# Capsule routing in a convolution kernel: one added on the scalar engine, exponentials behind copies, uniform votes behind pool taps, the ninth tap summed last in eight slots

## The reference

```python
def squash(s, axis=-1):
    n2 = jnp.sum(s * s, axis=axis, keepdims=True)
    return s * n2 / ((1.0 + n2) * jnp.sqrt(n2 + EPS))
...
    patches = patches.reshape(N, F_in, in_len, Ho, Wo, kh, kw)           # 4 input capsules of 8, 3x3 taps
    priors = jnp.einsum('nfdhwij,ofijud->nhwofiju', patches, weight)     # 4 output capsules of 8
    priors = priors.reshape(N, Ho, Wo, F_out, F_in * kh * kw, out_len)
    logits = jnp.zeros_like(priors)
    for r in range(3):
        probs = jax.nn.softmax(logits, axis=-3)                          # over the 4 output capsules
        out = jnp.sum(probs * priors, axis=-2, keepdims=True)
        if r != 2:
            out = squash(out)
            logits = logits + jnp.sum(priors * out, axis=-1, keepdims=True)
    out = squash(jnp.squeeze(out, axis=-2))
```

## Time and profile before

| | |
|---|---|
| median of 3 runs | 12398.2 us (12397.93 to 12406.01) |
| profiled execution: time, span | 12399.53 us, 12397.7 us |
| routing phase | first matmul of L708 at 85.7 us, last transfer out issued at 3824.76 us |
| busy over the span | PE 11867.1 us (96%), DVE 8639.8 (70%), ACT 7576.8 (61%), POOL 3955.4 (32%) |
| mean granted clock of TensorE | 0.987 of full speed |

### The profile page before, as it was taken

How to read it: one execution, slowest core, us unless ns; L and a number is a source line. 1 busy time by engine, 2 the same in 40 slices (tenths; PEclk the granted TensorE clock), 3 DMA queues, 4 the chain that set the end, 5 groups by cost and what they waited for, 6 DMA issues and landing times. The chain is left out here.

```text
span 12397.7 us, 255720 instructions
## 1 busy us (share of the span) xinstructions
PE 11867.1 (96%) x72764; PEld 4295.5 (35%) x72764; DVE 8639.8 (70%) x15928; ACT 7576.8 (61%) x15666; POOL 3955.4 (32%) x3876
## 2 busy tenths in 40 slices
PE   6999999999994999999999999999999999999899
PEld 2333333333331333333333333333333333333232
DVE  6777777777776777777777777777777777777300
ACT  4666666666662466666666666666666666666511
POOL 5777777777772010100101101011010010110144
PEclk9999999999996899999999999999999999999999
DMA  3110110110104333333333333333333333433365
GB/s 81 24 23 17 24 23 17 24 23 17 24 16 108 68 79 76 88 73 83 83 72 88 75 82 83 76 84 78 77 88 73 83 82 74 88 77 77 90 146 125
DMA packets 971114, 833.12 MB, mean 67 GB/s; under 512 B 669476, under 2 KB 703876, under 8 KB 960132
## 3 DMA queue, kind: packets, MB, share of 16 engines
q1 hardware_dynamic: 968196, 807.54, 29.6%
q10 hardware_dynamic: 1536, 8.39, 0.3%
HBM read 584.08 MB, written 229.48 MB: 66 GB/s over the span
## 5 line engine op out<-in xcount | busy, mean ns | idle before, releaser
L1616 DVE TENSOR_REDUCE a_big<-a_mp 128x1 f32<-128x512 f32 x8192 | 5181.0, 684 | 1933.2 <-PE a_mp L1453 1930.3
L1539 ACT ACTIVATE a_ex<-a_sc 128x512 f32<-128x512 f32 x8192 | 4393.9, 601 | 1718.6 <-PE a_sc L1441 1715.8
L1453 PE MATMUL a_mp<-a_ks,a_qs 108*128 108x512 bf16 x8192 | 3131.2, 383 | 40.1 <-DMA a_ks<-qk_parts 26.2
L1441 PE MATMUL a_sc<-a_qs,a_ks 111*128 111x512 bf16 x8192 | 3124.8, 383 | 45.4 <-issue 27.3
L928 DVE TENSOR_TENSOR r_prod<-r_pg,r_win 128x512 f32<-128x512 f32 x2816 | 1821.7, 684 | 775.5 <-PE r_pg L641 465.6
L550 POOL TENSOR_TENSOR r_prod<-r_temp,r_win 128x512 f32<-128x512 f32 x1792 | 2093.0, 1187 | 704.6 <-ACT r_temp L871 610.7
L1467 PE MATMUL a_po<-a_ex,a_va 128*32 128x512 f32 x16384 | 2216.7, 606 | 11.7 <-issue 6.3
L1441 PEld LDWEIGHTS a_sc<-a_qs,a_ks 111*128 111x128 bf16 x8192 | 795.8, 97 | 2593.0 <-ACT a_ex L1539 1747.0
L1352 POOL TENSOR_TENSOR a_on<-a_oc,a_zb 128x512 f32<-128x512 f32 x256 | 325.5, 1272 | 3508.3 <-DMA a_zb<-z_rows 3508.3
L1340 POOL TENSOR_TENSOR a_pieces<-a_left,a_pieces 128x512 bf16<-128x512 f32 x256 | 296.0, 1156 | 2900.4 <-ACT a_pieces L1525 2900.4
L871 ACT COPY r_temp<-r_pg 128x512 f32<-128x512 f32 x1792 | 976.8, 590 | 329.1 <-PE r_pg L641 207.8
(11 more groups left out here) (191 smaller groups left out, 10943.4 us busy)
## 6 DMA issues: line engine op xcount, KB each, us to landing
a_qs<-qk_parts SPq DMA_DIRECT2D x768, 144.0 KB
a_ks<-qk_parts SPq DMA_DIRECT2D x768, 144.0 KB
qk_parts<-a_pieces SPq DMA_DIRECT2D x128, 768.0 KB, 5.0
f_t<-mixed SPq DMA_DIRECT2D x48, 1536.0 KB, 16.1
a_tw<-second SPq DMA_DIRECT2D x512, 128.0 KB, 3.5
a_zb<-z_rows SPq DMA_DIRECT2D x256, 256.0 KB
mixed<-a_t SPq DMA_DIRECT2D x256, 256.0 KB, 5.8
r_win<-first SPq DMA_DIRECT2D x128, 280.5 KB, 5.0
```

Source lines behind the costliest of these rows:

```text
L1441: pe.matmul(sc[k % BANKS][:, :], ks[0:KROWS + NPART, p.h, head, 128 * kb:128 * kb + 128], qs[0:KROWS + NPART, p.h, head, CHUNK * qb:CHUNK ...
L1453: pe.matmul(mp[k % BANKS][:, :], qs[0:KROWS, p.h, head, 128 * q:128 * q + 128], ks[0:KROWS, p.h, head, CHUNK * half:CHUNK * half + CHUNK], ...
L1539: nc.scalar.activation(ex[:, k % RING, :], sc[k % BANKS][:, :], ACT.Exp, scale=scale).then_inc(exped.sem, 1)
L1616: nc.vector.tensor_reduce(big[:, x % 2, k // 2:k // 2 + 1], mp[k % BANKS][:, :], AX_X, ALU.max).then_inc(maxed.sem, 1)
```

## The change

It has four parts:

1. In the slots outside `FULLER` PE sums batch 2 ahead of batch 1, so tap 8 is last (`last_batches`); `when_summed` gives DVE and POOL the count to wait for before they overwrite a product.
2. In the squashes of rounds 1 and 2 ACT adds one to the squared norm, in part B ahead of Ln. DVE does reciprocal and ratio in part B, right ahead of L981, where they were in part A (`divide`). The uniform squash keeps its order on DVE.
3. The exponential of a softmax moves on ACT from the end of the slot of part A to part B, the slot after it, behind the copies of taps 4 and 5.
4. `first_votes` moves on POOL behind the products of taps 6 and 0 in slot 14. ACT's repeat of the first lane's vote moves from the end of slot 14 into slot 15, behind Ln and Exp and ahead of the copy out.

```diff
+def last_batches(s):
+    return (1, 2) if s % SLOTS in FULLER else (2, 1)
+
+def when_summed(s, g):
+    b = next(k for k, gs in enumerate(BATCHES) if g in gs)
+    return 3 * s + (1 + last_batches(s).index(b) if b else 0) + 1
...
@@ POOL
-            pool.wait_ge(reduced.sem, reduced.at(p.n, 3 * (s - 2) + batch_of[g] + 1))
+            pool.wait_ge(reduced.sem, reduced.at(p.n, when_summed(s - 2, g)))
...
-                elif r == 0:
-                    first_votes(n)
-                else:
+                elif r > 0:
                     scale_capsules(n, r, lane)
...
             for n, kind, r, lane in lit:
                 if kind == "softmax":
                     probabilities(n, r, lane)
+                elif r == 0:
+                    first_votes(n)
...
@@ PE
-                batch(behind.n, (s - 1) % SLOTS, 1)
-                batch(behind.n, (s - 1) % SLOTS, 2)
+                for b in last_batches(s - 1):
+                    batch(behind.n, (s - 1) % SLOTS, b)
...
@@ ACT
+                if r:
+                    nc.scalar.activation(fac[:, own, ls, :], norm[:, own, ls, :], ACT.Identity,
+                                         bias=one[:, 0:1]).then_inc(plus1[r].sem, 1)
                 nc.scalar.activation(lnorm[:, own, ls, :], norm[:, own, ls, :], ACT.Ln,
...
-            for d, kind, r, lane, part in lights(s, "B", ("squash",)):
+            for d, kind, r, lane, part in lights(s, "B"):
                 if d in which:
                     first_functions(p.to(d).n, kind, r, lane)
+            for d, kind, r, lane, part in back:
+                if r == 0 and lane == 0:
+                    repeat_votes(p.to(d).n, 0, 0)
...
-                if d in which and kind == "softmax":
-                    first_functions(p.to(d).n, kind, r, lane)
-                elif d in which and r == 0:
+                if d in which and kind == "squash" and r == 0:
                     uniform_capsules(p.to(d).n)
...
@@ DVE
+        def divide(n, r, lane):
+            k = lane + 1
+            nm, fc = (tile[:, int(r > 0), lanes_of(r, lane), :].rearrange("p l x -> p (l x)") for tile in (norm, fac))
+            dve.wait_ge(plus1[r].sem, plus1[r].at(n, k))
+            nc.vector.reciprocal(fc, fc).then_inc(recip[r].sem, 1)
+            dve.wait_ge(recip[r].sem, recip[r].at(n, k))
+            nc.vector.tensor_tensor(fc, fc, nm, ALU.mult).then_inc(ratio[r].sem, 1)
...
-                dve.wait_ge(normed[r].sem, normed[r].at(n, k))
-                nc.vector.tensor_scalar(fc, nm, 1.0, None, ALU.add).then_inc(plus1[r].sem, 1)
-                fill()
-                dve.wait_ge(plus1[r].sem, plus1[r].at(n, k))
-                nc.vector.reciprocal(fc, fc).then_inc(recip[r].sem, 1)
-                fill()
-                dve.wait_ge(recip[r].sem, recip[r].at(n, k))
-                nc.vector.tensor_tensor(fc, fc, nm, ALU.mult).then_inc(ratio[r].sem, 1)
+                if r == 0:
+                    dve.wait_ge(normed[r].sem, normed[r].at(n, k))
+                    nc.vector.tensor_scalar(fc, nm, 1.0, None, ALU.add).then_inc(plus1[r].sem, 1)
+                    divide(n, r, lane)
                 return
...
+            if r:
+                divide(n, r, lane)
```

More of the change, by code:

```diff
@@ L387, in routing_phase @@
     eps = sb("eps", [128, 1])
+    one = sb("one", [128, 1])
     prod = sb("prod", [128, TAPS, CHUNK])
@@ L418, in routing_phase @@
     pt = ctx.enter_context(nc.psum_tensor("r_pt", [128, CHUNK], F32))
-    batch_of = {g: b for b, gs in enumerate(BATCHES) for g in gs}
     fixed = sem("fixed")
@@ L682, in batch @@
                         last = pe.matmul(pl[C * q:C * q + C, cols], ws[:, 8, :], product_at(s, 8)[:, cols],
-                                         start=False, stop=False, tile_position=(0, C * q))
+                                         start=False, stop=b == last_batches(s)[1], tile_position=(0, C * q))
                 last.then_inc(reduced.sem, 1)
@@ L690, in batch @@
                     last = pe.matmul(pl[q:q + 32, :], ws[:, tap, :], rhs, start=b == 0,
-                                     stop=b == 2, tile_position=(0, q))
+                                     stop=b == last_batches(s)[1], tile_position=(0, q))
                 else:
@@ L780, in tail @@
         def tail(p):
-            batch(p.to(-1).n, SLOTS - 1, 1)
-            batch(p.to(-1).n, SLOTS - 1, 2)
+            for b in last_batches(SLOTS - 1):
+                batch(p.to(-1).n, SLOTS - 1, b)
         run_slots(pe, passes, slot, tail)
@@ L844, in second_functions @@
                 nc.scalar.activation(rz[:, lane, :], lz[:, lane, :], ACT.Exp, scale=-1.0).then_inc(rz_ready[r].sem, 1)
-            elif r < 2:
+            elif r == 1:
                 repeat_votes(n, r, lane)
@@ L905, in slot @@
             for d, kind, r, lane, part in lights(s, "A"):
-                if d in which and kind == "softmax":
-                    first_functions(p.to(d).n, kind, r, lane)
-                elif d in which and r == 0:
+                if d in which and kind == "squash" and r == 0:
                     uniform_capsules(p.to(d).n)
-                elif d in which:
+                elif d in which and kind == "squash":
                     square(p.to(d).n, r, lane)
@@ L920, in _ @@
         dve.wait_ge(fixed, 16 * 9)
+        nc.vector.memset(one[:, :], 1.0)
         nc.vector.memset(eps[:, :], SQUASH_EPS).then_inc(prepared, 1)
@@ L925, in product @@
             dve.wait_ge(made.sem, made.at(p.n, use + 1))
-            dve.wait_ge(reduced.sem, reduced.at(p.n, 3 * (s - 1) + batch_of[g] + 1))
+            dve.wait_ge(reduced.sem, reduced.at(p.n, when_summed(s - 1, g)))
             nc.vector.tensor_tensor(
```

## The result

The changed kernel takes 12294.4 us (median of 4 runs, 12281.7 to 12301.1) against 12400.5 us (12398.0 to 12406.0): ratio 0.9912, 95% interval 0.9896 to 0.9927. The prediction was 12288 us, with a range from 12238 to 12353.

The account below looks back on a forecast made before the run. PE was taken to bound the routing phase; 4.98 us gained less 1.54 given back is 3.44 us a pass, times 32 passes 110 us, so 12288 us, range 12238 to 12353.

Parts of the forecast that it names:

- L740's wait: PE's wait for POOL's probabilities goes, as POOL's chain starts about 0.8 us earlier: 0.20 us a pass gained.
- exponential ahead of a copy: Slots 2 and 10: the exponential delays a C copy that PE waits for, 0.25 us each, 0.50 us a pass lost.
- Identity, taken as covered: In slots 6 to 8 PE's makes were to hide ACT's added instruction, so no cost was counted there.
- It covers it, if its own products are there: Slots outside FULLER: batch 2, taking 1.0 us, covers PE's wait of at most 0.4 us if its products are ready earlier.
- L746's give-back: Slots 3, 4, 11 and 12: PE waits 0.17 us each for ACT's copy L889 behind the exponential, 0.68 us lost.
- 3 x 0.12: ACT's added Identity costs PE 0.12 us each in slots 0, 1 and 9: 0.36 us a pass lost.
- I take 0 for PE: DVE's division amid POOL's two products delays DVE at most 0.1 us and costs PE nothing.
- ACT does take part of the gain: Rival: copies behind exponential and Identity take over the removed waits; 12 us gained, 12386 us; chance of no change 0.08.
- all waits go: Rival: nothing new is late in PE's passes, 7.4 us a pass gained, 12161 us; chance of over 160 us gain 0.06.
- the swap the only part that works: Rival: only summing tap 8 last gains, the rest cancels; 64 us, 12334 us, inside the forecast's range, no separate chance.
- DVE does not fall behind POOL: Denies the rival: L981 waits one more POOL instruction in eight slots, 82 us slower, 12480; chance 0.10 with any loss.
- a give-back of 0.4 us: Low end of the assumed give-back, 0.4 to 3.5 of 4.98 us, paired with a gain of 45 to 160 us.

Follow-up runs that it names:

- part 2 alone: The kernel before the change, with only ACT adding one and DVE dividing in part B: 12397.9 us, ratio 0.9992.
- part 4 alone: The kernel before the change, with only the uniform votes behind POOL's products and the vote's repeat in slot 15: 12387.4 us, ratio 0.9987.

## Why the prediction was right

The mechanism was right: PE's waits for L967, for tap 8, for POOL and for the probabilities went, and ACT's copies became what PE waits for. That the total is so close is in part luck, as the terms show. By slots, with the 3.44 us of the sum divided among them:

| slots | terms | predicted | measured |
|---|---|---|---|
| 3, 4, 5, 11, 12, 13 | parts 1 and 3, less L746 | 2.65 | 3.29 |
| 6 | part 2, and L740's wait | 1.30 | 1.25 |
| 2, 10 | exponential ahead of a copy | -0.50 | -0.51 |
| 1, 9 | Identity | -0.24 | -0.38 |
| 7, 8 | Identity, taken as covered | 0 | -0.17 |
| 15, 0 | part 4 less Identity | 0.23 | 0.02 |

- **Part 1**, 1.99 us. The waits went as worked out, but alone it gave 1.32 us by the slots. "It covers it, if its own products are there" was right; what was not asked is what PE meets next, ACT's copies. In the whole change part 3 meets this.
- **Part 3**, 1.34 us. Slots 5 and 13 gave 1.33 us alone. It also gave 0.41 us in slot 6, which overlaps with part 2's 1.10: together slot 6 is 1.25 us shorter.
- **L746's give-back**, 4 x 0.17. Moving the exponential behind L905 shortened each of slots 3, 4, 11 and 12 by 0.13 us, which is this term as measured. It doesn't appear in the list of PE's waits, where the prediction looked for it; the only listed wait of L756 is the one in slot 9.
- **Identity**, 3 x 0.12. It is 0.21 us on ACT: the pace of L815 to its next instruction is not that of an activation ahead of Ln. And it was put in the wrong slots. The 44 waits for L856 lie in slots 1 and 2, not 0 and 1, and slot 2 has no Identity. It is paid in slots 1, 9 and 7, 0.47 us by the kernel without it. Slot 8's 0.08 us stays there without Identity, and its cause is not shown.
- **Part 4**, 0.35 us, was not there in the whole change. Slot 15 is 0.19 us shorter and slot 0 0.17 us longer. Alone part 4 gives 0.47 for the two and part 2 alone takes 0.59, more than the 0.12 of Identity. The step that failed is "I take 0 for PE": it looked at the slots where the division stands beside POOL's products, and not at slot 14, where it stands ahead of DVE's last products. With part 4 alone ACT's copies start at +1.23 and L729 at +3.80. In the whole change the copies start at +1.50, since the square ahead of them waits for DVE, which is 0.27 us, and Identity adds 0.21: the transpose starts at +4.24, and the gain is gone. That ACT is next in line, with L729 at +3.97, was right in kind.
- **Rivals.** ACT does take part of the gain (PE's waits for the copy out are 2.33 us a pass), but far from all. Of the 7.4 us that "all waits go" needed less than half came. Nor is the swap the only part that works: part 3 gives as much. DVE does not fall behind POOL: L1002 grew to 1.10 us as the prediction expected, by the median of 288. Here the rule of the Trainium skill (SBUF — State Buffer, Who interferes with whom) on two SBUF inputs that was weighed there agrees with the trace, with L1002 ending with POOL's product; the rival that rested on it fell because POOL waits for this result itself.

So errors of both signs cancel: 0.64 us too little in slots 3 to 5 and 11 to 13, 0.52 too much in slots 1, 7, 8, 9, 15 and 0. The range has a slip too: a give-back of 0.4 us leaves 4.58 us a pass or 147 us, so its far end, 160 us, means that nothing at all is given back.

## What to carry to other kernels

Where one engine bounds a loop with a fixed order of instructions, look for its waits in the length of its groups as well as in its idle time, and remove a wait together with what would be late 0.3 us behind it: parts 1 and 3 are worth 3.20 us a steady pass together, where each alone gives 1.32 and 1.47. Then go to the engine that serves the bounding one and sort its queue by who waits first; here some 51 us (12294.4 to 12243.4, not run side by side; 1.79 us a pass) lay in ACT's order alone. An instruction put on that queue is cheap only while the queue has slack: the first 0.21 us cost 0.47 us over eight slots, 0.42 more cost 2.66.

When you divide a gain among parts, read neighbouring slots together. Slot 15 alone says that part 4 works in the whole change; slots 15 and 0 say that it does not.

## What the runs showed of the hardware

An activation of 16 columns costs 0.21 us on ACT when the next is independent of it (three in a row in the timeline above). A DVE product of 16 columns with both inputs in SBUF takes 0.17 us alone and 1.10 us in the median where it stands beside POOL's products (L1002). The add, with one input tile in SBUF, is stretched as well (L997, 0.66 us in the median, 0.16 at the least), and the reciprocal between them is not, 0.25 us in each row shown. How many of them there are mattered little here, since POOL stops for the last: without the add they ended with POOL's second product, with it 0.24 us behind.
